# Expert results gathered with an add, transfers spread over steps, slots worked out inside units, throw-away matmuls in the last units

## The chip, the cores and the metric

The kernel runs on one core of a Trainium2 chip. The metric is the device time of the whole launch in microseconds. The core has TensorE (PE in the profile), VectorE (DVE), ScalarE (ACT), GpSimd (POOL) and the queues of DMA transfers that SyncE (SP), ACT and POOL issue.

## The reference

x has 4 sequences of 1024 rows of 128. The result is x + attention(xn) + experts(xn), with xn the layer norm of x.

```python
xn = _layernorm(x)
# attention: 16 heads of 8, rotary embedding, causal softmax, output projection Wo
# experts, 8 of them, 512 wide:
probs = softmax(xn @ router_w.T); top_w, top_idx = top_k(probs, 2)
top_w = top_w / (sum(top_w) + 1e-09)
y_e = relu(xn @ w1[e].T + b1[e]) @ w2[e].T + b2[e]
out = sum over the two chosen experts of top_w * y_e
```

All of it is in float32.

## The kernel before

**Start.** x is loaded and normalised into `xn_all`, transposed, projected to q, k, v and to the router's logits, for the four sequences in turn. DVE then chooses two experts per row (L937 to L947) and computes their shares and the gates (L949 to L954). PE counts the tokens of each expert (`count_tokens`), and DVE turns the counts into the slot of every row in a list sorted by expert, each expert's part rounded up to whole tiles of 128 rows (L1098 to L1124). The list has 72 tiles, in DRAM (`slots_in_d`).

**Units.** Attention is cut into 16 units, one per sequence and group of four heads. `unit(u, r)` on each engine walks through 12 steps, a step being one block of 128 keys against one half (512) of the queries: 4 steps for the first half, 8 for the second. In step j PE makes the scores of step j + 2 (L1271), ACT their exponentials into one of three tiles `probs` (L764), POOL masks the diagonal block in steps 0 to 3 and 8 to 11 (L660), and PE makes the products with the values (L1306). In between, `plan_items` spreads 20 items of the maximum search of the next two units: PE makes raw scores (L1237), DVE takes their maxima (L874, L882). After step 6 DVE joins the maxima, PE transposes them in step 7 (`turn_max`, `TURN` is 7), DVE copies them out (L991) and SP stores them as two more rows of the next unit's stack (`store_max_rows`, L418). DVE copies the head results out at steps 3 and 11 (L997).

**Transfers in units.** POOL scatters the 64 blocks of 128 rows of xn (32 blocks, two experts each) into their slots with indirect DMAs (L634), in units 0 to 11. The table `SCATTERS` says how many stand behind which of the eight masks: three behind the mask of step 3 in units 0 to 3, two in units 4 to 11, and some single ones.

**Experts.** Behind unit 11 (`LAST` is 12) the 72 tiles run: SP loads a tile, PE transposes it (L1364), multiplies with the expert's first weights (L1355), ACT and DVE add the bias and clip, PE multiplies with the second weights (L1373), DVE copies the result (L1062), and SP stores it (L536). PE and ACT have made the first two steps of unit 12 before that. At tiles 0, 3, 68 and 70 SP loads x anew into `acc`, which is the memory of `xn_all` (`load_acc`, `ACC_AT`). POOL waits for all stores of results in `before_last`, ahead of unit 12.

**Units 12 to 15.** POOL gathers the results back, 64 indirect DMAs of 128 rows into eight tiles `got` (L643, table `TRANSFERS`, up to 12 of them behind the mask of step 3), and waits before each for the combine of eight earlier. DVE multiplies each with its share and adds it to `acc` (`combine`, L1029, table `COMBINES`). Sums and heads of the sequences are spread and multiplied (`invert_sums`, `finish_heads`), PE projects them in unit 15 (`project`, L1396, L1410), DVE adds the projection to `acc` (L1045), and SP stores.

**Warm matmuls.** `keep_warm(n, to)` issues n matmuls whose result nobody reads (L1159); `WARM` has their numbers at six places of the start.

## Time and profile before

| | us |
|---|---|
| median of 3 runs | 768.5 |
| lowest, highest | 759.3, 769.29 |
| profiled execution, as timed | 764.56 |
| its span in the profile | 762.8 |
| PE busy | 696.3 |
| DVE busy | 582.2 |
| ACT busy | 444.4 |
| POOL busy | 254.8 |

Busy is the time with an instruction of the engine under way. PE's pipelined matmuls make its figure an upper one. "Idle before" names what ended an engine's idle time; "issue" and "remote" mean that the profile shows no wait that explains it.

### The profile page before, as it was taken

To read this page: it belongs to the slowest core of one execution; us is meant where nothing else is said; L and a number is where in the kernel's file an instruction comes from. 1 tells how busy PE (TensorE), PEld (TensorE's weight loads), DVE (VectorE), ACT (ScalarE), POOL (GpSimd) and SP (SyncE) were. 2 spreads that over 40 slices of the span, in tenths; PEclk is the share of its full clock that TensorE was granted. 3 is DMA by queue.
4 is the path that set the end of the run, shared out by engine and by line. 5 is a ranking of instruction groups with operands and counts; after the bars stand their busy time and mean duration, and the time that the engine had idled before them with its cause. 6 is when DMAs were issued, how large, how long until landed. Compare 5 with 4: busy or idle time off the path is not lost. (4 is left out here: it accounts for less than half of the span.)

```text
span 762.8 us, 18457 instructions
## 1 busy us (share of the span) xinstructions
PE 696.3 (91%) x6064; PEld 398.4 (52%) x6064; DVE 582.2 (76%) x1337; ACT 444.4 (58%) x962; POOL 254.8 (33%) x308
## 2 busy tenths in 40 slices
PE   8799898999999999999999997999999779788887
PEld 3456343434434444444444447999999624343434
DVE  6956978879879889889889884666666559797344
ACT  3455024666666677677677675666666346556541
POOL 2556212424334333433523520000000146565821
PEclk9999998999999999999999998999999869898989
DMA  8499950236355255134225413222222521111654
GB/s 222 129 231 231 236 100 20 45 78 102 73 116 100 60 96 80 38 54 79 50 45 77 63 32 95 78 69 69 69 69 69 135 52 38 46 34 40 162 126 130
DMA packets 64621, 69.36 MB, mean 91 GB/s; under 512 B 9934, under 2 KB 52430, under 8 KB 64490
## 3 DMA queue, kind: packets, MB, share of 16 engines
q1 hardware_dynamic: 60458, 60.08, 36.2%
q0 software_dynamic: 4096, 8.40, 4.2%
q8 instruction: 40, 0.66, 0.4%
q14 instruction: 27, 0.22, 0.1%
HBM read 41.11 MB, written 26.67 MB: 89 GB/s over the span
## 5 line engine op out<-in xcount | busy, mean ns | idle before, releaser
L764 ACT ACTIVATE probs<-bank 128x512 f32<-128x512 f32 (+2 forms) x640 | 314.8, 555 | 214.0 <-PE bank L1271 185.1
L882 DVE TENSOR_REDUCE mx<-bank 128x2 f32<-128x1024 f32 (+2 forms) x200 | 220.6, 1130 | 51.1 <-PE bank L1245 33.8
L1271 PE MATMUL bank<-stack 64*128 64x512 f32 (+3 forms) x768 | 196.4, 439 | 25.8 <-issue 16.0
L660 POOL TENSOR_SCALAR_AFFINE_SELECT probs<-probs 128x512 f32<-128x512 f32 x128 | 81.1, 635 | 406.7 <-ACT probs L764 253.6
L1306 PE MATMUL bank<-probs,vst 128*32 128x256 f32 (+2 forms) x2560 | 199.6, 387 | 5.0 <-POOL probs L660 5.0
L1271 PEld LDWEIGHTS bank<-stack 64*128 64x128 f32 x768 | 89.9, 189 | 157.5 <-issue 77.7
L1237 PE MATMUL bank<-stack 64*128 64x512 f32 (+3 forms) x768 | 149.2, 382 | 6.1 <-DVE mx L882 4.0
L874 DVE CUSTOM_DVE_ANT_0 q_high<-bank,later_s 128x384 bf16<-128x384 f32 (+1 forms) x240 | 135.1, 619 | 9.5 <-PE bank L1237 8.0
L1306 PEld LDWEIGHTS bank<-probs,vst 128*32 128x32 f32 x2560 | 52.2, 110 | 88.9 <-issue 72.7
L1237 PEld LDWEIGHTS bank<-stack 64*128 64x128 f32 x768 | 78.0, 193 | 39.1 <-issue 19.6
L1355 PE MATMUL bank<-tiles_s,staged 128*128 128x128 f32 x576 | 78.3, 280 | 0.7 <-ACT tiles_s L768 0.7
L1373 PE MATMUL bank<-staged,q_high 128*128 128x128 f32 x576 | 76.2, 275 | 0.5 <-DVE k_high L1062 0.5
L643 POOL DMA_INDIRECT k_high<-slots_out_d,slot x64 | 61.3, 958 | 40.6 <-DVE xn_all L1029 27.3
L1355 PEld LDWEIGHTS bank<-tiles_s,staged 128*128 128x128 f32 x576 | 71.4, 195 | 1.4 <-ACT tiles_s L768 1.4
L1373 PEld LDWEIGHTS bank<-staged,q_high 128*128 128x128 f32 x576 | 70.0, 192 | 0.7 <-issue 0.6
L778 ACT COPY staged<-early 128x516 f32 x72 | 44.8, 622 | 42.8 <-DVE q_high L1071 41.4
L634 POOL DMA_INDIRECT slots_in_d<-xn_all,slot x64 | 62.6, 977 | 12.8 <-issue 12.8
L1071 DVE TENSOR_SCALAR q_high<-bank,staged 128x128 f32<-128x128 f32 x144 | 43.9, 346 | 23.7 <-PE bank L1355 20.4
L789 ACT ACTIVATE q_high<-bank,staged 128x128 f32<-128x128 f32 x144 | 44.6, 360 | 1.6 <-PE bank L1373 1.1
L1062 DVE COPY k_high<-bank 128x128 f32<-128x128 f32 x72 | 21.0, 292 | 27.7 <-PE bank L1373 27.7
L997 DVE COPY xnT<-bank 128x512 f32<-128x512 f32 x32 | 22.0, 687 | 17.4 <-remote 10.3
L1159 PE MATMUL bank<-ones_b 128*128 128x512 bf16 x122 | 32.1, 415 | 1.1 <-POOL ones_b L586 1.1
(137 smaller groups left out, 477.4 us busy)
## 6 DMA issues: line engine op xcount, KB each, us to landing
stack<-parts_d SPq DMA_DIRECT2D x96, 128.0 KB
slots_in_d<-const_s SPq DMA_DIRECT2D x4, 1152.0 KB, 10.5
tiles_s<-slots_in_d SPq DMA_DIRECT2D x72, 64.0 KB, 1.8
slots_out_d<-k_high SPq DMA_DIRECT2D x72, 64.0 KB, 1.6
early<-in_w_experts SPq DMA_DIRECT2D x8, 514.0 KB
stack<-parts_d SPq DMA_DIRECT2D x64, 64.0 KB
parts_d<-probs SPq DMA_DIRECT2D x8, 512.0 KB, 6.1
heads_d<-xnT SPq DMA_DIRECT2D x124, 18.0 KB
```

The lines of the kernel that those rows point to most:

```text
L634: pool.indirect_dma_start(out=slots_in_d, out_offset=bass.IndirectOffsetOnAxis(ap=slot[:, k2, t:t + 1], axis=0), in_=xn_all[:, t, :], in_o ...
L643: pool.indirect_dma_start(out=got[n % GOT], out_offset=None, in_=slots_out_d, in_offset=bass.IndirectOffsetOnAxis(ap=slot[:, k2, t:t + 1], ...
L660: pool.affine_select(out=t, in_=t, compare_op=ALU.is_ge, fill=0.0, base=0, pattern=[[0, HG], [1, P]], channel_multiplier=-1).then_inc(s["d ...
L764: nc.scalar.activation(to, src, ACT.Exp, scale=SCALE).then_inc(s["probs_made"], 1)
L778: nc.scalar.copy(w_s[r % 2][:, 0:F + FC], early[:, bass.ds(e * WIDE, F + FC)]).then_inc(s["w1_staged"], 1)
L874: last = v.tensor_tensor_reduce(hidden_scores[n % 2 * 2 + g][:, 0:w], ms[(r * MI + n) % 2][:, g * HALF:g * HALF + w], later_s[:, HALF - w: ...
L882: v.tensor_reduce(to, src.rearrange("p g (a k) -> p g a k", k=w), AX_X, ALU.max, negate=True).then_inc(s["scores_read"], 1)
L1237: last = mm(at[:, col:col + w], qstk[r][g][:, hp, qb * P:(qb + 1) * P], kstk[r][g][:, hp, c * HALF:c * HALF + w], start=not both or i == 0 ...
L1271: made = mm(st_of(u, n, i)[:, col:col + HALF - q0], kstk[r][g][:, hp, kb * P:(kb + 1) * P], qstk[r][g][:, hp, c * HALF + q0:(c + 1) * HALF ...
L1306: last = mm(pv[32 * h:32 * h + 32, begin:end], vst[r % 2][:, kb, h, :], probs[n % 3][:, h, begin:end], start=kb == 0 and begin == 0, stop= ...
L1355: last = mm(at[:, col:col + P], w_s[r % 2][:, f * P:(f + 1) * P], xtT[r % 2], start=True, stop=True)
L1373: last = mm(pv[:, 0:C], hid[r % 2][:, f * P:(f + 1) * P], w_s[r % 2][:, F + FC + f * C:F + FC + (f + 1) * C], start=f == 0, stop=f == FC - 1)
```

## The change

- *Adding gathers.* The share of each row travels with the row: `xn_all` becomes the first 128 columns of `rows_s`, whose column 129 holds the share. `put_share(0)` fills it for the first expert's scatters and `put_share(1)`, in unit 6, for the second's. DVE's copy of an expert's result multiplies with that column. The gathers add into `acc` themselves (`compute_op=ALU.add`); `combine`, `got` and the semaphore `combined` go. The gather of a row's second expert waits until that of the first has landed, and `add_projection` waits for the gathers of its sequence (`results_added`).
- *Paced transfers.* POOL waits at every step, not at masked ones alone, for the step's probabilities, and `SCATTERS` and `TRANSFERS` have an entry for each of 12 steps: one scatter per step in units 2 to 11, two gathers per step in steps 3 to 8 of units 12 to 15. The wait for all stored results stands before the first gather.
- *Slots in units.* The chain from the counts to the slots, the shares and the gates runs in pieces (`rank`) behind the reads of steps 7 to 10 of units 0 to 3 and 6. The transposes of the gates (`turn_gates`) move to the front of the experts.
- *Tile loads.* The first four stand in unit 11, before the store of the second half's heads. A later tile is loaded behind the store of the tile before, three ahead.
- *Maximum rows of unit 0.* Half of them are stored on ACT's queue.
- *Throw-away matmuls.* `WARM` is smaller at two places; there is one behind each early score of unit 0, three at the experts' front, three before the last `turn_max`, and two at most steps from (14, 8) on (`FILLS`).

```diff
@@ -313,7 +314,7 @@
-        WARM = [30, 45, 1, 10, 22, 6]
+        WARM = [30, 35, 1, 10, 12, 6]
@@ -320,16 +321,18 @@
+        FILLS = {**{(LAST + 2, j): (7, 0) for j in range(TURN + 1, NS)}, **{(LAST + 3, j): (7, 0) for j in range(5)},
+                 **{(LAST + 3, j): (4, 1) for j in range(6, 8)}, **{(LAST + 3, j): (7, 2) for j in range(9, NS)}}
-        INVERTS = {4: 0, 5: 1, 7: 2}
+        INVERTS = {8: 0, 9: 1, 10: 2}
-        SCATTERS = [[1, 0, 0, 3, 1, 0, 0, 1]] * 4 + [[1, 0, 0, 2, 1, 0, 0, 1]] * 8
+        SCATTERS = ([[0] * 12] * 2 + ([[0, 0, 0, 1, 1, 1, 1, 1, 1, 0, 0, 1]] * 4 + [[0, 0, 1, 1, 1, 1, 0, 0, 0, 0, 0, 0]]) * 2)
-        TRANSFERS = [[1, 0, 0, 11, 2, 1, 0, 2]] * 2 + [[1, 0, 0, 12, 2, 1, 0, 2]] + [[1, 0, 0, 9, 2, 0, 0, 0]]
-        COMBINES = [[0, 0, 1, 0, 1, 2, 3, 3, 2, 1, 1, 1], [0, 1, 1, 0, 2, 2, 3, 3, 2, 1, 1, 1],
-                    [0, 1, 1, 0, 2, 3, 3, 3, 2, 1, 1, 1], [1, 1, 1, 0, 1, 2, 2, 2, 2, 1, 1, 0]]
+        TRANSFERS = [[0, 0, 0, 2, 2, 2, 2, 2, 2, 1, 1, 2], [1, 0, 0, 2, 2, 2, 2, 2, 2, 1, 1, 2],
+                     [1, 0, 0, 2, 2, 2, 2, 2, 2, 1, 1, 2], [1, 1, 1, 2, 2, 2, 2, 2, 1, 0, 0, 0]]
...
@@ -348,7 +351,7 @@
-            return n // 4 * 2 + n % 2, n // 2 % 2
+            return n // 8 * 4 + n % 4, n // 4 % 2
...
+                if isinstance(u, int) and u == LAST - 1:
+                    sp.wait_ge(s["scattered"], 16 * 2 * NT)
+                    for j in range(4):
+                        load_tile(j, j)
                 store_heads(u, 1)
...
             def tile(j, r):
                 if past(j):
                     store_tile(j - 1, (r - 1) % 4)
-                if not isinstance(j, int) or j + 4 < TILES:
-                    sp.wait_ge(s["xT_made"], j + 1)
-                    load_tile(j + 4, r)
+                    if not isinstance(j, int) or j + 3 < TILES:
+                        load_tile(j + 3, (r + 3) % 4)
...
             def gather(n):
                 t, k2 = gather_order(n)
-                if n >= GOT:
-                    pool.wait_ge(s["combined"], n - GOT + 1)
-                pool.indirect_dma_start(out=got[n % GOT], out_offset=None, in_=slots_out_d,
+                if n == 0:
+                    for r in range(4):
+                        pool.wait_ge(y_stored[r], 16 * TILES // 4)
+                if k2 == 0:
+                    pool.wait_ge(acc_loaded[t // T], 16)
+                else:
+                    pool.wait_ge(gathered[(n - 4) % GOT], 16 * ((n - 4) // GOT + 1))
+                pool.indirect_dma_start(out=acc[:, t, :], out_offset=None, in_=slots_out_d,
                                         in_offset=bass.IndirectOffsetOnAxis(ap=slot[:, k2, t:t + 1], axis=0),
+                                        compute_op=ALU.add).then_inc(gathered[n % GOT], 16)
...
+                    else:
+                        pool.wait_ge(s["probs_made"], banks_before(u, n + 1))
+                    if u < LAST:
+                        for i in share_of(SCATTERS, u, n):
+                            scatter(i)
+                    else:
+                        for i in share_of(TRANSFERS, r, n):
+                            gather(i)
...
@@ -1059,7 +1057,7 @@
-                v.tensor_copy(yst[r % 4], pv[:, 0:C]).then_inc(s["y_copied"], 1)
+                v.tensor_scalar(yst[r % 4], pv[:, 0:C], tile_rows[:, r % 4, C:C + 1], None, ALU.mult).then_inc(s["y_copied"], 1)
...
+            def rank(u, j):
+                if (u, j) == (0, TURN):
+                    first_slots()
+                if (u, j) == (0, TURN + 1):
+                    next_slots()
+                if (u, j) == (0, TURN + 2):
+                    places()
+                if (u, j) == (1, TURN):
+                    slots_of(0)
+                if (u, j) == (1, TURN + 2):
+                    slots_of(1)
+                if (u, j) == (1, TURN + 3):
+                    share_out()
+                    put_share(0)
+                if (u, j) == (6, TURN + 2):
+                    put_share(1)
+                if (u, j) == (2, TURN + 2):
+                    gates_out()
+                if (u, j) == (3, TURN):
+                    expert_tiles()
+                if (u, j) == (3, TURN + 2):
+                    expert_ends()
...
                     if j == TURN and more(u, 1):
+                        if not more(u, 2):
+                            pe.wait_ge(s["scores_read"], UNITS * MI - 2)
+                            keep_warm(3, 7)
                         turn_max(u + 1, (r + 1) % 4)
                     second_products(r, j)
+                    if (u, j) in FILLS:
+                        to, read = FILLS[u, j]
+                        pe.wait_ge(s["scores_read"], UNITS * MI + read)
+                        keep_warm(2, to)
...
@@ -1386,8 +1456,11 @@
                 turn_tile(0, 0)
+                turn_gates()
+                keep_warm(3, 7)
                 all_tiles(pe, tile)
...
@@ -1433,11 +1506,13 @@
-            pe.wait_ge(s["gT_kept"], 1)
+            pe.wait_ge(s["scores_read"], MI + AT_START)
             for n in range(LEAD):
                 for h in range(HG):
                     score(0, 0, n, h)
-            pe.wait_ge(s["routed"], 1)
+                    if n or h:
+                        keep_warm(1, 7)
+            pe.wait_ge(s["counts_kept"], 2)
```

## Rows read from the trace of the kernel before

**Rows 1.** The page: the span, and the granted clock in 40 slices

```profile
span 762.8 us, 18457 instructions
...
PEclk9999998999999999999999998999999869898989
```

**Rows 2.** Busy time by unit: length, PE, PEld, DVE, ACT, POOL, clock, DMA

```profile
147.70:177.90 30.20, 28.19 (x275) 12.41 (x274) 24.73 (x53) 19.64 (x41) 11.21 (x15) 0.94 0.39 74
177.90:206.70 28.80, 26.79 (x278) 12.19 (x277) 24.54 (x53) 19.71 (x41) 11.27 (x16) 1.00 0.56 98
206.70:236.90 30.20, 28.27 (x277) 12.57 (x276) 24.77 (x53) 19.67 (x41) 11.23 (x16) 0.94 0.45 91
...
320.20:347.80 27.60, 26.74 (x274) 12.15 (x273) 24.51 (x53) 19.54 (x41) 10.24 (x15) 1.00 0.38 59
...
607.20:646.50 39.30, 33.71 (x273) 14.14 (x273) 27.68 (x59) 18.71 (x39) 22.58 (x27) 0.80 0.27 49
646.50:682.30 35.80, 29.41 (x274) 13.14 (x274) 31.48 (x73) 20.13 (x41) 21.70 (x27) 0.90 0.17 43
682.30:716.70 34.40, 28.11 (x234) 11.80 (x233) 24.10 (x59) 19.79 (x40) 22.09 (x27) 0.90 0.24 61
716.70:752.30 35.60, 31.05 (x257) 16.00 (x256) 12.45 (x22) 15.88 (x32) 15.68 (x19) 0.90 0.64 160
...
461.80:603.30 141.50, 139.65 (x1225) 138.64 (x1225) 92.37 (x287) 93.60 (x286) 0.00 (x0) 0.99 0.27 78
```

**Rows 3.** Order of time, third scatter of unit 1: start, length, [idle before]

```profile
154.28 0.96 POOL L634 DMA_INDIRECT slots_in_d<-xn_all,slot  x1 [0.30 <-issue]
...
156.07 0.69 DVE L997 COPY xnT<-bank 128x512 f32<-128x512 f32 x1 [1.04 <-remote]
```

**Rows 4.** Order of time, second and last scatter of unit 4

```profile
242.24 0.96 POOL L634 DMA_INDIRECT slots_in_d<-xn_all,slot  x1 [0.30 <-issue]
```

**Rows 5.** Order of time, gathers of unit 14 beside DVE, ACT and PE

```profile
690.21 0.95 POOL L643 DMA_INDIRECT k_high<-slots_out_d,slot  x1 [0.30 <-issue]
...
692.19 0.69 DVE L997 COPY xnT<-bank 128x512 f32<-128x512 f32 x1 [1.54 <-remote]
...
692.88 1.33 ACT L764 ACTIVATE probs<-bank 128x512 f32<-128x512 f32 x2 [2.68 <-remote]
...
693.53 0.49 PE L1271 MATMUL bank<-stack 64*128 64x512 f32 x1 [2.79 <-issue]
```

**Rows 6.** Page, gathers: busy, mean ns, idle before; and the combines alone

```profile
L643 POOL DMA_INDIRECT k_high<-slots_out_d,slot x64 | 61.3, 958 | 40.6 <-DVE xn_all L1029 27.3
...
L1029 DVE SCALAR_TENSOR_TENSOR xn_all<-k_high,share,xn_all x64: 253/344/731, 618.1 to 752.0; 128x128 f32<-128x128 f32 x64
```

**Rows 7.** Order of time, end of the start

```profile
86.25 0.18 DVE L949 SCALAR_TENSOR_TENSOR r_s<-share 128x32 f32<-128x32 f32 x1
...
89.06 0.42 DVE L957 COPY tiles_s<-bank 128x256 f32<-128x256 f32 x1 [0.60 <-PE bank L1219]
...
98.11 2.55 PE L1159 MATMUL bank<-ones_b 128*128 128x512 bf16 x11
...
101.30 0.41 DVE L1098 COPY staged<-bank 128x256 f32<-128x256 f32 x1
...
101.46 2.50 SPq L418 DMA_DIRECT2D stack<-mrow  x4
...
106.83 0.73 PE L1271 MATMUL bank<-stack 64*128 64x512 f32 x3
...
109.02 0.20 DVE L1124 TENSOR_SCALAR expert<-xnT 128x72 int32<-128x72 f32 x1
```

**Rows 8.** Order of time, experts' first transpose; chain, a later load

```profile
461.03 0.45 PE L1364 MATMUL bank<-const_s,tiles_s 128*128 128x128 f32 x1 [3.49 <-DMA tiles_s<-slots_in_d]
...
474.98 3.05 DMA tiles_s<-slots_in_d
```

**Rows 9.** Order of time, unit 12's first products

```profile
607.18 1.08 PE L1306 MATMUL bank<-probs,vst 128*32 128x256 f32 x8 [3.21 <-POOL probs L660]
```

**Rows 10.** Chain of waits, the last gathers of unit 15

```profile
743.87 6.74 DMA k_high<-slots_out_d,slot
```

More of the change, by code:

```diff
@@ L795, in experts @@
                 act.wait_ge(s["experts_loaded"], 16 * E)
+                act.wait_ge(s["expert_known"], 1)
                 stage_w1(0, 0)
@@ L1124, in _, with put_share @@
[L1124 to L1128 removed]
+                if n:
+                    dve.sem_inc(s["routed"], 1)
+            def put_share(n):
+                if n:
+                    dve.wait_ge(s["scattered"], 16 * NT)
+                v.tensor_copy(rows_s[:, :, C], share[:, n, :]).then_inc(s["shared"], 1)
```

189 lines of the change are left out of this document (93 added, 96 removed).

## The prediction

> **What bounds the kernel now.** I read the page first, then the busy time unit by unit, then the order of instructions where a unit is long, and last the two stretches in which one stage hands over to the next. The page says that the profiled execution took 762.8 us of span, and its clock line has dips behind the expert stage [rows 1]. The unit-by-unit view shows what matters most. Unit 7 takes 27.6 us with TensorE (PE) busy 26.74, VectorE (DVE) 24.51, GpSimd (POOL) 10.24 and the clock at 1.00: PE bounds a steady unit. Units 12, 13 and 14 take 39.3, 35.8 and 34.4 us for the same products, at clocks of 0.80 and 0.90 (of the full 2.4 GHz), and unit 15 takes 35.6. Units 1, 2 and 3 take 30.2, 28.8 and 30.2. The 72 expert tiles take 141.5 us between unit 11 and unit 12, with PE busy 139.65 [rows 2].
>
> What makes units 1 to 3 and 12 to 14 long is seen where POOL issues transfers in a row. In unit 1 a third scatter starts at 154.28 and DVE's copy of the heads, which waits for PE's fourth step, comes only at 156.07, after 1.04 us in which what it waited for should long have been done [rows 3]. In unit 4 only two scatters stand there, and nothing is late [rows 4]. In unit 14 gathers follow each other every 1.25 us; ACT sits for 2.68 us and PE for 2.79 us right behind them [rows 5]. After such a hold the clock falls to 1.2 GHz for a stretch, which is how unit 14 comes to a mean of 0.90. Units 12 to 14 also carry 64 combines of 344 ns on DVE [rows 6]; unit 13 has DVE busy 31.48 us [rows 2], more than a steady unit lasts. Both are causes, and the trace doesn't separate them.
>
> **The change part by part.** The sum is made against the profiled execution, 764.56 us as it was timed (762.8 of span and 1.8 around it). The median of the runs shown is 768.5, four above it.
>
> *Before the first unit.* The share and gate work, from L949 at 86.25 to L957's end at 89.48, leaves DVE's path: 3.2 us, of which PE still needs some for the counts and its first item. I take 2.1. The four stores of the maximum rows are 2.50 us of SP's queue [rows 7]; two of them move to ACT's queue, so the last is issued 1.2 earlier. Together -3.3 (0 to -4.4). The slot work behind (L1098 to L1124, 101.30 to 109.22) runs beside PE's warm matmuls and the wait for those rows until 106.83 [rows 7], so its going gives nothing more. The warm matmul that now follows each early score is 0.23 us (2.55 by 11) [rows 7]; seven of them lie behind ACT's exponentials. Unit 0 has 18 score reads in its first seven steps and is DVE's; I leave it.
>
> *The same work inside units 0 to 3 and 6.* 3.2 plus 7.9 us, some 11 us of DVE, go into units in which DVE has 27.6 less 24.5, or 3.1 us free [rows 2]. The pieces stand at steps 7 to 11, where PE next waits for DVE's reads. None of it may show, or all 11 may; units 0 and 1 get most of it, over 3 us each. I take +4.
>
> *Scatters one per step.* A scatter occupies POOL for some 0.96 us [rows 4] and one alone or two in a row delay nothing. Units 1 to 3 lose their excess over 27.6: 2.6, 1.2 and 2.6 [rows 2], -6.4 (0 to -6.4). The 64 scatters now stand one to a step in units 2 to 11, seven in a full unit, where POOL has 17 us free. The wider rows (129 columns for 128) I cost at nothing: they hide behind PE, and a tile load now is issued two tiles, 3.8 us, before its turn; without that cover each of 72 tiles would show it.
>
> *Entering the experts.* PE's first tile starts at 461.03 after 3.49 us of waiting for the first tile's load [rows 8]. The loads move into unit 11, ahead of SP's store of heads. Two transposes and three warm matmuls come in, about 1.1. So -2.4. One later load took 3.05 behind the 512 KB load of x [rows 8]; the acc loads remain, and I take -1 (0 to -2). Scaling the result by its weight in DVE's copy is hidden: PE is busy 139.65 of 141.5 [rows 2].
>
> *Leaving the experts.* PE waits 3.21 us before the first products, since POOL held the mask of step 0 until all results were stored [rows 9]. That wait moves to the first gather, at step 3, behind the masks: -3.2. Late next are the gathers, and nobody wants those before unit 15.
>
> *Units 12 to 15.* Over three steady units, units 12 to 14 have 39.3 + 35.8 + 34.4 - 82.8 = 26.7 us too much [rows 2]. The combines go (64 times 0.344, 22 us of DVE), and so does POOL's waiting for them, 27.3 us [rows 6]. What stays: POOL. A gather is 0.96 plus 0.3, 1.25 us [rows 5]; 17 a unit make 21.3, and with masks and the v copy (10.24 less five scatters, 5.4) 26.7 of 27.6 us. It fits, barely, and now waits at each step for its probabilities, which can push a mask late. I take +2 for each of three units, +6. In units 14 and 15, 31 warm matmuls of 0.23 are 7.2 us of PE, about half of it where PE waits anyway: +3. The second gather of a row waits for the first to land. Under load one took 6.74 us [rows 10], and two steps are some 4.6: +2. Unit 15 is 35.6 with three projections in it; I give it -2. So -26.7 - 2 + 6 + 3 + 2 = -17.7.
>
> Sum: -3.3 + 4 - 6.4 - 2.4 - 1 - 3.2 - 17.7 = -30.0, and 764.6 less 30 is 735 (-4.4% on the median).
>
> The largest term rests on how POOL's transfers and PE disturb each other. The row shows PE sitting for 2.79 us beside a run of gathers [rows 5]. The Trainium skill (SBUF — State Buffer, Who interferes with whom) says the opposite: PE and ACT never wait on anyone, and DMA has ports of its own. By the rows pacing is worth most of 26.7 and 6.4; by the rule it is worth nothing in itself, and only the combines' departure counts. The rule is a rival below.
>
> **The accumulating gather** is not in the trace. Its nearest row is the plain gather, 958 ns [rows 6]. From below it costs that. From above I take twice, 1.9 us (plus the 0.3 between two), since it names the same rows and each row is read twice, once from each side. I take the plain price: POOL writes one list of 128 rows either way.
>
> **The rivals.**
>
> *A, the run remains a run.* Two gathers at each of six steps of 2.2 to 2.5 us are again one every 1.25 us, so PE can be held as in unit 14. For: the cadence is that of [rows 5]. Against: nothing but POOL's short waits between pairs. A hold of 2.8 and its slow-clock stretch (a clock of 0.90 over 34.4 us is 6.9 us at 1.2 GHz, at most 3.4 us lost) are 5 to 6 us a unit, less the 2 already in the sum: +11, 746. If also the lone scatter that now falls on PE's fourth step holds it by 1.2 in nine units, 757.
>
> *B, everything is hidden.* No late masks, no cost of the slot work: -6 - 4, so 725; with fills and landings hidden, 720.
>
> *C, gathers don't disturb PE.* Pacing then gives nothing: units 1 to 3 keep their 6.4, and units 12 to 14 gain what DVE loses, 17 combines of 0.344, 5.9 us each, 17.6, without the other terms of POOL. -3.3 + 4 - 2.4 - 1 - 3.2 - 17.6 + 3 = -20.5: 744. For: DVE's 31.48 in unit 13 [rows 2]. Against: DVE too sat idle there, 1.54 us [rows 5].
>
> *D, slower: the accumulating gather is dear.* POOL is full at 1.3 us per gather. Each further 0.1 costs 64 of them 6.4 us. It eats the 30 us from 1.3 + 30/64, some 1.8 us on, and is slower by 2% from 2.1. At 1.9 + 0.3 the sum is 735 + 0.9 x 64, or 793. Masks are the victims: steps 8 to 11 and 0 to 3 would wait for POOL.
>
> **How the numbers follow.** Forecast 735 (728 to 741): 0.38. A (742 to 757): 0.25. B (below 728): 0.19. C (744): 0.08. D: 0.10. The range takes the forecast, A, B and C whole: 715 to 757. Two per cent is about what a measurement of this kernel tells from no change; faster by that is below 753. So faster 0.84, same 0.08, slower 0.08.
>
> **What would show it.** Right: units 1 to 3 near 27.6; units 12 and 13 under 31 at a clock near 1.00; first products right behind the last result; gathers of 0.96 us in pairs. Wrong: a gather row well above 1 us (D); ACT and PE idle together at the fourth step beside gathers (A); units 0 and 1 longer by 3 us at steps 7 to 11 (the slot work). My largest doubt is the 2 us per unit for late masks.

## The result, and the profile after

| | before | after |
|---|---|---|
| median of the runs made together | 768.9 us (4 runs) | 785.9 us (4 runs) |
| span of the profiled execution | 762.8 us | 791.6 us (timed as 793.4) |

The changed kernel is slower: the ratio of the mean times is 1.026, 95% interval 1.017 to 1.036, so whether it is slower by as much as 2% stays open. Medians and ratios below are of the fast runs, since a slow execution of the same kernel takes some per cent longer. The page's first lines say where to look: a clock that is lower behind the experts than before (compare [rows 1]), nearly three times the packets in GpSimd's queue for the same kind of gather, gathers of 1575 ns for 958 [rows 6], and, in the chain of waits, the load of an expert tile at 4%, which has 1% in the page of the kernel before.

Page of the kernel after: span, granted clock, GpSimd's queue, chain by line, gathers:

```profile
span 791.6 us, 18396 instructions
...
PEclk9999967998999999999999999999999986959799
...
q0 software_dynamic: 11264, 8.43, 6.7%
...
PE bank L1369 6%; PE bank L1443 5%; PE bank L1334 5%; DMA k_high<-slots_in_d 4%; POOL rows_s L655 2%; PE bank L1300 2%; ACT q_high L795 2%; PE bank L1425 2%; ACT probs L770 2%; PE bank L1434 2%; ACTq L778 1%; SPq L541 1%; PE bank L1218 1%; DVE k_high L1060 1%; PE bank L1469 1%
...
L655 POOL DMA_INDIRECT rows_s<-slots_out_d,slot x64 | 100.8, 1575 | 20.1 <-issue 11.0
```

Kernel after, busy time by stretch, columns as in [rows 2]: units 1, 2, 3 and 7, then from unit 11's last product to unit 12's first (the experts with the way in and out), then units 12 to 15:

```profile
152.70:182.40 29.70, 27.06 (x273) 12.30 (x273) 27.44 (x63) 20.11 (x42) 6.18 (x11) 1.00 0.40 62
182.40:213.10 30.70, 29.73 (x273) 13.19 (x274) 25.96 (x56) 18.69 (x39) 11.64 (x16) 0.89 0.50 94
213.10:241.30 28.20, 27.03 (x273) 12.29 (x274) 25.82 (x56) 19.57 (x41) 12.79 (x17) 1.00 0.55 100
324.70:352.40 27.70, 26.83 (x276) 12.17 (x276) 24.63 (x53) 19.63 (x41) 12.21 (x17) 1.00 0.39 64
461.20:628.60 167.40, 153.22 (x1249) 142.10 (x1242) 95.86 (x296) 102.38 (x293) 1.27 (x2) 1.00 0.26 68
628.60:666.80 38.20, 29.21 (x278) 13.06 (x277) 25.45 (x56) 20.66 (x42) 29.63 (x25) 0.85 0.45 62
666.80:706.60 39.80, 36.06 (x273) 15.69 (x273) 26.43 (x51) 18.84 (x39) 32.58 (x27) 0.71 0.29 39
706.60:745.10 38.50, 33.00 (x248) 12.79 (x248) 19.88 (x38) 20.33 (x42) 31.46 (x27) 0.78 0.53 103
745.10:780.90 35.80, 33.53 (x275) 16.84 (x276) 7.35 (x7) 14.58 (x30) 27.83 (x21) 1.00 0.56 116
```

The same stretch between unit 11 and unit 12 of the kernel before:

```profile
456.60:607.20 150.60, 141.72 (x1245) 139.72 (x1238) 95.62 (x299) 97.09 (x294) 0.62 (x1) 0.97 0.28 80
```

So the 28.8 us of span divide like this: the first product of unit 0 is 3.2 later (115.4 for 112.2); units 0 to 11 add 1.4; the expert stretch adds 16.8 (167.4 for 150.6); units 12 to 14 add 7.0 (116.5 for 109.5); unit 15 and what follows 0.4. Two things had no term in my sum, the expert stretch growing and the gathers' price.

**Where the expert stretch grows.** The kernel after in order of time, one turn of the tile loop, first on SyncE's queue, then on PE:

```profile
541.71 0.35 SPq L541 DMA_DIRECT2D slots_out_d<-k_high  x1
542.26 0.34 SPq L537 DMA_DIRECT2D k_high<-slots_in_d  x1
...
542.29 0.32 PE L1434 MATMUL bank<-const_s,k_high 128*128 128x128 f32 x1 [0.36 <-ACT q_high L795]
542.57 1.13 PE L1443 MATMUL bank<-staged,q_high 128*128 128x128 f32 x8
543.53 1.06 PE L1425 MATMUL bank<-tiles_s,staged 128*128 128x128 f32 x8
544.43 0.27 PE L1434 MATMUL bank<-const_s,k_high 128*128 128x128 f32 x1
```

L541 stores the result of tile j - 1, L537 behind it loads tile j + 3. The transpose of that tile (L1434) is the one at 544.43: 2.2 us later, and that only since the pitch (the time from one tile to the next) has already grown. A tile load lands 1.8 us after its issue (the page, in both kernels). What the lead would be at the old pitch of 1.9 us can be read from the trace of the kernel before: from the place behind the store of tile j - 1, 0.55 us after that store's issue, to the transpose of tile j + 3 there are 1.54 us (median of tiles 10 to 59; 1.48 to 1.57). That is less than the landing takes, so the loop can't keep its pitch: 58 tiles pass between 470 and 600 us where 68 did before. The lead that the kernel before really gives its loads, four tiles ahead, is 3.44 us in the median; in the kernel after it is 2.06.

**Where units 12 to 14 grow.** Step 7 of these units takes 9.3, 6.3 and 6.3 us where a steady unit has 3.2. Kernel after, unit 13, GpSimd and then PE:

```profile
688.46 1.55 POOL L655 DMA_INDIRECT rows_s<-slots_out_d,slot  x1 [0.30 <-ACT probs L770]
690.32 1.57 POOL L655 DMA_INDIRECT rows_s<-slots_out_d,slot  x1 [0.30 <-ACT probs L770]
691.29 1.25 POOL L672 TENSOR_SCALAR_AFFINE_SELECT probs<-probs 128x512 f32<-128x512 f32 x1
...
692.68 0.79 PE L1369 MATMUL bank<-probs,vst 128*32 128x256 f32 x8 [3.40 <-POOL probs L672]
```

PE stands for 3.40 us for the mask of step 8, and the mask stood behind ten gathers. They come every 1.84 to 1.86 us; the plain ones came every 1.25 [rows 5]. (The mask's record begins inside the last gather's and ends 0.65 us after it, so its 1.25 us are 0.63 of work and the rest of waiting; before it has 0.63. POOL's busy time in the windows above counts such an overlap once, so it is not too large by it.)

### The profile page after: what moved, and what is told of

It is laid out like the page before. It is cut to its first block and busy times, and to the rows that moved or that the text cites. A ratio compares the mean times of both kernels' runs of the same rounds, so it can differ in the third digit from the quotient of the medians.

```text
span 791.6 us, 18396 instructions
## 1 busy us (share of the span) xinstructions
PE 722.3 (91%) x6085; PEld 404.9 (51%) x6085; DVE 565.2 (71%) x1276; ACT 449.8 (57%) x962; POOL 296.1 (37%) x308
## 3 DMA queue, kind: packets, MB, share of 16 engines
q1 hardware_dynamic: 60394, 60.14, 35.4%
q0 software_dynamic: 11264, 8.43, 6.7%
## 5 line engine op out<-in xcount | busy, mean ns | idle before, releaser
L672 POOL TENSOR_SCALAR_AFFINE_SELECT probs<-probs 128x512 f32<-128x512 f32 x128 | 95.8, 763 | 370.3 <-ACT probs L770 369.2
L1369 PE MATMUL bank<-probs,vst 128*32 128x256 f32 (+2 forms) x2560 | 201.8, 391 | 21.0 <-POOL probs L672 19.4
L1334 PEld LDWEIGHTS bank<-stack 64*128 64x128 f32 x768 | 90.7, 194 | 141.6 <-ACT probs L770 68.1
L887 DVE CUSTOM_DVE_ANT_0 q_high<-bank,k_high 128x384 bf16<-128x384 f32 (+1 forms) x240 | 135.2, 620 | 12.5 <-PE bank L1300 10.2
L655 POOL DMA_INDIRECT rows_s<-slots_out_d,slot x64 | 100.8, 1575 | 20.1 <-issue 11.0
L1300 PEld LDWEIGHTS bank<-stack 64*128 64x128 f32 x768 | 79.1, 199 | 40.4 <-issue 18.3
L641 POOL DMA_INDIRECT slots_in_d<-rows_s,slot x64 | 62.2, 973 | 57.2 <-ACT probs L770 52.7
L1443 PE MATMUL bank<-staged,q_high 128*128 128x128 f32 x576 | 79.6, 281 | 0.5 <-DVE k_high L1060 0.5
L1425 PE MATMUL bank<-tiles_s,staged 128*128 128x128 f32 x576 | 76.2, 275 | 0.4 <-ACT tiles_s L774 0.4
L1060 DVE TENSOR_SCALAR k_high<-bank,k_high 128x128 f32<-128x128 f32 x72 | 25.3, 351 | 51.2 <-PE bank L1443 51.2
L1218 PE MATMUL bank<-ones_b 128*128 128x512 bf16 x143 | 43.8, 435 | 1.1 <-POOL ones_b L587 1.1
```

What stands on the lines that cost most here:

```text
L641: pool.indirect_dma_start(out=slots_in_d, out_offset=bass.IndirectOffsetOnAxis(ap=slot[:, k2, t:t + 1], axis=0), in_=rows_s[:, t, :], in_o ...
L655: pool.indirect_dma_start(out=acc[:, t, :], out_offset=None, in_=slots_out_d, in_offset=bass.IndirectOffsetOnAxis(ap=slot[:, k2, t:t + 1], ...
L672: pool.affine_select(out=t, in_=t, compare_op=ALU.is_ge, fill=0.0, base=0, pattern=[[0, HG], [1, P]], channel_multiplier=-1).then_inc(s["d ...
L887: last = v.tensor_tensor_reduce(hidden_scores[n % 2 * 2 + g][:, 0:w], ms[(r * MI + n) % 2][:, g * HALF:g * HALF + w], later_s[:, HALF - w: ...
L1300: last = mm(at[:, col:col + w], qstk[r][g][:, hp, qb * P:(qb + 1) * P], kstk[r][g][:, hp, c * HALF:c * HALF + w], start=not both or i == 0 ...
L1334: made = mm(st_of(u, n, i)[:, col:col + HALF - q0], kstk[r][g][:, hp, kb * P:(kb + 1) * P], qstk[r][g][:, hp, c * HALF + q0:(c + 1) * HALF ...
```

## The experiments

All ratios are to the kernel before as it ran beside them. "Stretch" is from unit 11's last product to unit 12's first. Besides before and after, twelve kernels ran.

| kernel | ratio, 95% interval | stretch | units 12 / 13 / 14 | unit 15, to its last step |
|---|---|---|---|---|
| before | 1 | 150.6 | 39.3 / 35.8 / 34.4 | 35.1 |
| after | 1.026 (1.017 to 1.036) | 167.4 | 38.2 / 39.8 / 38.5 | 35.4 |
| plain_gather | 1.014 (1.005 to 1.022) | 170.2 | 40.4 / 33.6 / 34.7 | 38.1 |
| early_tile_loads | 0.984 (0.977 to 0.990) | 146.0 | 38.4 / 39.0 / 38.4 | 35.1 |
| old_start | 1.024 (1.017 to 1.031) | 170.1 | 37.6 / 37.3 / 38.5 | 34.5 |
| before_paced | 0.972 (0.965 to 0.978) | 146.0 | 33.9 / 36.9 / 35.4 | 33.1 |
| spread_adds | 1.022 (1.013 to 1.032) | 165.6 | 36.7 / 37.7 / 38.1 | 35.0 |
| after_repaired | 0.990 (0.986 to 0.995) | 143.9 | 36.5 / 36.7 / 37.7 | 35.1 |
| no_fills | 1.021 (1.012 to 1.031) | 167.7 | 38.4 / 39.0 / 38.1 | 34.6 |
| gathers_apart | 0.990 (0.983 to 0.997) | 145.2 | 34.0 / 35.4 / 29.4 | 47.1 |
| repaired_plain | 0.981 (0.973 to 0.990) | 144.1 | 33.8 / 34.8 / 36.6 | 33.4 |
| paced_apart | 0.979 (0.970 to 0.987) | 146.0 | 34.0 / 33.9 / 32.1 | 32.9 |
| paced_inverts | 0.982 (0.973 to 0.990) | 145.7 | 35.7 / 37.5 / 35.4 | 31.4 |
| before_late_loads | 1.023 (1.009 to 1.038) | 172.9 | 38.2 / 35.7 / 35.9 | 38.8 |

### The late tile load: early_tile_loads, before_late_loads

early_tile_loads puts the load back to its old place. The weight then no longer lies in the row when the result is copied, so the copy multiplies by a constant column:

```diff
-                    if not isinstance(j, int) or j + 3 < TILES:
-                        load_tile(j + 3, (r + 3) % 4)
+                if not isinstance(j, int) or j + 4 < TILES:
+                    sp.wait_ge(s["xT_made"], j + 1)
+                    load_tile(j + 4, r)
...
-                v.tensor_scalar(yst[r % 4], pv[:, 0:C], tile_rows[:, r % 4, C:C + 1], None, ALU.mult).then_inc(s["y_copied"], 1)
+                v.tensor_scalar(yst[r % 4], pv[:, 0:C], eps_s[:], None, ALU.mult).then_inc(s["y_copied"], 1)
```

> The changed kernel with the tile loads issued as before: four tiles ahead, behind the transpose that frees the buffer. The weight column would be overwritten too early, so the copy multiplies by a constant column instead (the experts' weights are left out of the result); its cost stays. Theory L (in the changed kernel the load is issued so late that PE's transpose of the tile waits for its landing, 1.8 us): the expert stage goes from 167.6 us between the last products of unit 11 and the first of unit 12 to 145 to 150, total lower by 17 to 22 us. Rival M (the copy with a multiply or the rows of 129 columns slow the stage): it stays over 160, total within 1% of the changed kernel.

The stretch falls by 21.4 us and the ratio from 1.026 to 0.984: the kernel now takes less time than the one before, by 1.6%. (The median is 27 us below the changed kernel's, more than the 17 to 22 expected.) Rows of 129 words and the scaled copy (351 ns for 292) are still in it, so these cost nothing that shows.

before_late_loads is the other direction, this one move alone in the kernel before:

```diff
-                if not isinstance(j, int) or j + 4 < TILES:
-                    sp.wait_ge(s["xT_made"], j + 1)
-                    load_tile(j + 4, r)
+                    if not isinstance(j, int) or j + 3 < TILES:
+                        load_tile(j + 3, (r + 3) % 4)
```

> The kernel before with one thing of the change alone: in the experts the load of tile j + 3 behind the store of tile j - 1, instead of the load of tile j + 4 behind the transpose of tile j. Rows of 512 bytes, gathers, slots and start as before. Theory L (the load is issued only some 1.6 us before its transpose at the old pitch, and takes 1.8 us and more to land, so the pitch of a tile goes from 1.9 to about 2.2 us): from unit 11's last product to unit 12's first it takes 170 to 173 us instead of 150.6, and the kernel takes 785 to 790 us, 2.7 to 3.1% above the kernel before. Rival X (it needs the change's other parts too, the row of 129 words whose landing is longer, or the scaled copy of 351 instead of 292 ns in front of the store): 151 to 158 us there, 766 to 774 us in all.

The stretch grows by 22.3 us and the ratio is 1.023. Nothing else of the change is needed; rival X is out. PE's transpose in before_late_loads, grouped from 470 to 600 us (count, busy us and mean ns, idle before and releaser):

```profile
L1363 PE MATMUL bank<-const_s,tiles_s 128*128 128x128 f32 x59 | 18.4, 312 | 4.8 <-DMA tiles_s<-slots_in_d 3.5 <-ACT q_high L788 0.6
```

The same group in the kernel before, which differs from it by this move alone:

```profile
L1364 PE MATMUL bank<-const_s,tiles_s 128*128 128x128 f32 x68 | 18.6, 273 | 0.6 <-DMA tiles_s<-slots_in_d 0.6
```

59 transposes against 68 in the same 130 us. The idle time put down to the load is small, 3.5 us, and yet the load costs 22: a late transpose delays ACT's copy and that the next tile's first products, and a wait on that chain is booked under other names. The stage's length shows the cost, the wait's row does not.

### The adding gather: plain_gather, spread_adds, after_repaired, repaired_plain

plain_gather takes the sum away from the changed kernel (each gather overwrites; the sums are left out):

```diff
-                                        in_offset=bass.IndirectOffsetOnAxis(ap=slot[:, k2, t:t + 1], axis=0),
-                                        compute_op=ALU.add).then_inc(gathered[n % GOT], 16)
+                                        in_offset=bass.IndirectOffsetOnAxis(ap=slot[:, k2, t:t + 1], axis=0)).then_inc(gathered[n % GOT], 16)
```

> The changed kernel with one thing undone: the gathers don't add, they overwrite (the sums of expert results are left out). All waits and places stay. Theory G (the adding gather is what makes units 12 to 14 long: 1549 ns on POOL for 958 before, so the mask of step 8 comes late): gathers fall to about 0.96 us, step 7 of units 12 to 14 from 9.3, 6.3 and 6.3 us to about 3.1, units 12 to 14 from 38.2, 39.8 and 38.5 us to 28 to 30, total lower by 22 to 28 us. Rival H (a run of gathers one every 1.25 us holds PE at the fourth step whatever the gathers do): gathers are short, but step 3 takes 5 to 6 us again, units 33 to 34, total lower by 10 to 15. Rival F (the warm matmuls and waits for landings make them long): no change beyond 1%.

Gathers are 944 ns again (median) and the holds at step 7 shrink from 9.3, 6.3 and 6.3 us to 4.4, 3.1 and 2.9, but units 12 to 14 only fall from 116.5 to 108.7 us, because other holds come: 6.6 us at step 6 of unit 12, 6.7 at step 5 of unit 14. The whole gains 1.2% with intervals that overlap. So theory G's 22 to 28 us didn't come, and not even rival H's 10 to 15, though long steps beside runs of gathers are what H is about.

spread_adds keeps the sum and takes the ten gathers in five steps apart:

```diff
-        TRANSFERS = [[0, 0, 0, 2, 2, 2, 2, 2, 2, 1, 1, 2], [1, 0, 0, 2, 2, 2, 2, 2, 2, 1, 1, 2],
-                     [1, 0, 0, 2, 2, 2, 2, 2, 2, 1, 1, 2], [1, 1, 1, 2, 2, 2, 2, 2, 1, 0, 0, 0]]
+        TRANSFERS = [[1, 1, 1, 1, 2, 2, 1, 1, 1, 2, 2, 1], [1, 1, 1, 1, 2, 2, 2, 1, 1, 2, 2, 1],
+                     [1, 1, 1, 1, 2, 2, 2, 1, 1, 2, 2, 1], [1, 1, 1, 1, 2, 2, 2, 1, 1, 2, 0, 0]]
```

> The changed kernel with another table of gathers: one in the steps 0 to 3 and 8, two in the steps 4 to 6, where POOL has no masks, 16 to 17 in a unit instead of 16 to 18, and no ten in the five steps 3 to 7. Experts and all else as in the changed kernel. Theory S (the adding gather's 1.55 us is dear only because ten of them stand in a row in front of the mask of step 8): POOL has 17 x 1.6 + 8 masks x 0.6 = 32 us of work in a unit and PE's own is 34, so the hold at step 7 (6.3 to 9.3 us of a step) goes, units 12 to 14 take 34 to 35.5 us each instead of 38.2, 39.8 and 38.5, and the time falls by 10 to 13 us to 773 to 776. Theory F (POOL is full, the place doesn't matter): the hold turns into smaller ones at other masks, units 12 to 14 stay at 37 to 39 us each, and the time is 782 to 788.

The hold at step 7 shrinks to 3.8 to 4.5 us and steps 9 and 10 become 4.1 and 4.2: 112.5 us in place of 116.5, and no gain in the ratio that can be told. Theory F holds: POOL is all but full. The table has 16, 17 and 17 gathers in units 12, 13 and 14 (the 18 in the expectation is one too many). 17 at 1.84, eight masks at 0.63 and the v copy of 0.39 are 36.7 us, and units 13 and 14 take 37.7 and 38.1; besides the 0.3 us between two gathers POOL's idle time in them is 2.0 and 1.9 us. By this only fewer gathers in a unit could shorten it, which was not tried with adding ones.

after_repaired is spread_adds with the early load made right: VectorE copies the weight to a tile of its own, behind which the row may be overwritten:

```diff
+            def keep_weight(j, r):
+                dve.wait_ge(s["xT_made"], j + 1)
+                if not isinstance(j, int) or j >= 4:
+                    dve.wait_ge(s["y_copied"], j - 3)
+                v.tensor_copy(weights[:, r % 4:r % 4 + 1], tile_rows[:, r % 4, C:C + 1]).then_inc(s["weight_kept"], 1)
...
                 if following:
                     stage_w2(j + 1, r + 1, e)
+                    keep_weight(j + 1, r + 1)
```

> The same table of gathers, and the tile loads four ahead again behind the transpose as before, with the weight's column copied by VectorE to a small tile of its own, so that the scaled copy still multiplies the right weight. Theory S with theory L (the late tile load costs the experts 20 to 27 us): the experts take 142 to 147 us and units 12 to 14 take 34 to 35.5 each; 745 to 750 us, 2.5 to 3% below the kernel before. Theory F with L: 755 to 760. If the wider row itself (516 instead of 512 bytes) or the small copies cost something, experts come out above 147 us, as early_tile_loads (145.9) had both the wide rows and no small copies.

759.0 us, ratio 0.990, against 1.022 for spread_adds beside it: a stretch of 143.9 us for 165.6. Against the kernel before that is no difference of 2%. The 72 small copies (148 ns each) hide. With theory F I had expected 755 to 760; this is all of the change, repaired.

repaired_plain is that kernel with plain gathers (sums left out again):

> after_repaired with the gathers plain again (the sums are left out: every gather overwrites the row of x, so this is a price and no kernel to use). The traces so far show an adding gather every 1.84 us when POOL has nothing else to do (1.54 of the gather, 0.3 to the next) and a plain one every 1.25. Theory F (POOL is full in units 12 to 14: 18 x 1.84 + 8 masks x 0.63 + 0.4 = 39 us in the changed kernel): with plain gathers POOL needs 17 x 1.25 + 5.4 = 27 us, its idle time comes back, the steps of 4.1 to 4.5 us at 7, 9 and 10 fall to 2.1 to 3.2, units 12 to 14 take 32 to 34.5 us each instead of 36.5, 36.7 and 37.7; 745 to 752 us. Theory R (runs of plain gathers hold PE, as in plain_gather, whose units 12 to 14 took 40.4, 33.6 and 34.7): the table has at most six gathers in three steps, so one step of 4 us or more stays in every unit, at 5 to 6, and the time is 752 to 758.

750.8 us; units 12 to 14 take 105.2 us for 110.9 and unit 15 33.4 for 35.1. So the adding costs 7.4 us in these units; the ratios, 0.981 and 0.990, give the same 7 with intervals that overlap. POOL has room now, but steps of 5.3, 5.5 and 6.0 us stand at 7, 5 and 5: theory R has its part (the time lies in F's range, the long steps and unit 14 in R's). Busy time of units 12 and 14 in after_repaired; POOL's number, the last but three, is what to look at:

```profile
605.40:641.90 36.50, 31.70 (x277) 13.93 (x277) 25.69 (x52) 20.08 (x41) 30.95 (x26) 0.82 0.47 66
...
678.60:716.20 37.60, 31.05 (x245) 12.26 (x244) 19.52 (x37) 19.54 (x41) 32.60 (x26) 0.82 0.52 99
```

The same units in repaired_plain:

```profile
597.90:631.70 33.80, 30.17 (x276) 13.38 (x275) 24.28 (x51) 19.76 (x41) 21.62 (x27) 0.90 0.37 70
...
666.50:703.10 36.60, 32.51 (x245) 12.93 (x244) 18.84 (x38) 19.30 (x40) 20.85 (x26) 0.83 0.25 61
```

### Pacing by itself: before_paced, gathers_apart, paced_apart, paced_inverts

before_paced is the kernel before (plain gathers, combines on VectorE, its own start) with at most two transfers in a row, the wait for the results moved from all masks to the first gather, and the first four tile loads in unit 11:

```diff
-        SCATTERS = [[1, 0, 0, 3, 1, 0, 0, 1]] * 4 + [[1, 0, 0, 2, 1, 0, 0, 1]] * 8
+        SCATTERS = [[1, 0, 0, 2, 1, 1, 0, 1]] * 4 + [[1, 0, 0, 2, 1, 0, 0, 1]] * 8
-        TRANSFERS = [[1, 0, 0, 11, 2, 1, 0, 2]] * 2 + [[1, 0, 0, 12, 2, 1, 0, 2]] + [[1, 0, 0, 9, 2, 0, 0, 0]]
+        TRANSFERS = [[0, 0, 0, 2, 2, 2, 2, 2, 2, 1, 1, 2], [1, 0, 0, 2, 2, 2, 2, 2, 2, 1, 1, 2],
+                     [1, 0, 0, 2, 2, 2, 2, 2, 2, 1, 1, 2], [1, 1, 1, 2, 2, 2, 2, 2, 1, 0, 0, 0]]
```

> The kernel before, with plain gathers and combines kept, and these parts of the change: at most two scatters in a row, gathers two per step at the places of the changed kernel, POOL's wait for all results at the first gather, the first four tile loads in unit 11. The combines follow two steps behind their gathers. Theory P (pacing removes PE's hold, and the two hand-overs save their waits of 3.5 and 3.2 us): units 12 to 14 take 29 to 31 us, units 1 to 3 27.6 to 28.8, total 738 to 746. Rival H (the cadence of one gather every 1.25 us holds PE anyway): step 3 of units 12 to 14 stays at 5 us and more, total 755 to 762. Rival C (DVE with its combines is the bound): units 12 and 13 at 32 or more without a long step 3, total 748 to 755.

750.3 us, ratio 0.972: faster than both kernels. Units 1 to 3 take 27.9, 27.6 and 27.6 us, the stretch 146.0, units 12 to 14 106.1 for 109.5. None of the three theories fits whole: P's 29 to 31 us a unit are missed, H's long step 3 is not there, and C's numbers are met (units over 32 without a long step 3, 748 to 755). But what makes the units long is a hold at step 5 of units 13 and 14 (6.7 and 6.8 us), and C's reason, the combines, doesn't explain it: repaired_plain has no combines and has it too (5.5 and 6.0). before_paced in unit 13: PE's last full pair of scores before the hold, the last of six gathers in a row, then ACT, PE and DVE:

```profile
646.91 0.50 PE L1274 MATMUL bank<-stack 64*128 64x512 f32 x2
...
649.40 0.94 POOL L648 DMA_INDIRECT k_high<-slots_out_d,slot  x1 [0.30 <-issue]
650.40 1.09 ACT L767 ACTIVATE probs<-bank 128x512 f32<-128x512 f32 x2 [3.12 <-remote]
...
651.05 0.75 PE L1274 MATMUL bank<-stack 64*128 64x512 f32 x1 [2.41 <-ACT probs L767]
...
651.73 2.36 DVE L885 TENSOR_REDUCE mx<-bank 128x2 f32<-128x1024 f32 x2 [2.76 <-remote]
```

ACT's input is made by the pair of PE's matmuls of 646.91, which by their rows end at 647.41, 3.0 us before ACT starts. But the profile models a matmul's end, and it records apart from that when a semaphore is raised, the counter by which PE tells ACT that the scores are there. In this trace a score matmul's semaphore rises 0.01 us after the modelled end (median). For this pair it rose at 650.32 and 650.35, and for the products before them (modelled end 646.98) at 650.29; ACT starts at 650.40. So ACT isn't late on an input that is there: it gets PE's word 2.9 us late, and DVE too starts (651.73) right behind a semaphore of PE's (651.70). PE's own wait of 2.41 us, for ACT, comes only after. Whether PE's matmuls themselves stood or only their word did, the trace doesn't tell.

The same can be looked for in all fourteen traces: exponentials that start more than 0.9 us late, with ACT free, their scores made by the modelled end and their buffer free. The eight traces with plain gathers have 52 of them, and in 49 ACT starts within 0.11 us of a semaphore of PE's. The six with adding gathers have none over 0.11 us.

gathers_apart puts one gather in each step of units 12 to 14 and the other 28 in unit 15; the combines follow two steps behind:

```diff
+        TRANSFERS = [[1] * 12] * 3 + [[3, 3, 3, 3, 3, 3, 3, 3, 3, 1, 0, 0]]
+        COMBINES = [[0, 0, 1, 1, 1, 1, 1, 1, 1, 1, 1, 1]] + [[1] * 12] * 2 + [[1, 1, 3, 3, 3, 3, 3, 3, 3, 3, 3, 1]]
```

> before_paced with one gather in every step of units 12 to 14 and the other 28 in unit 15, three in a row; the combines two steps behind. Theory G (a run of plain gathers, one per 1.25 us, holds PE for 2.5 to 3 us when it has gone on for about five of them; a gather that stands alone doesn't): units 12 to 14 have no step of 6.7 us, take 32 to 33.5 us each instead of 33.9, 36.9 and 35.4, and unit 15 has the hold, more than one perhaps. Theory M (the hold is not the gathers but what else lies at those steps: masks, stacks, head stores): a step of over 6 us stays in units 13 and 14 at the same place. The total isn't what this run is for: POOL has 28 x 1.0 us in unit 15 and its last gathers land late; 745 to 756 us.

The three units take 98.7 us for 106.1, 34.0, 35.4 and 29.4 each where theory G had 32 to 33.5, and none of those late semaphores of over 0.9 us is in them; unit 15 has three, of 2.9, 1.3 and 7.9 us. That is what G says. (The units also have fewer gathers and combines than before; repaired_plain's holds without any combine speak against the combines.) The one long step, 5.9 us at step 7 of unit 13, has another cause: PE waits 1.99 us for VectorE's maxima, which stand behind the three reciprocals of the sums (0.94 to 0.96 us each). Unit 15 pays with 47.1 us and one step of 10.9, so the whole gives the gain back.

paced_apart takes a middle way, 15, 15, 16 and 18 gathers, twos with ones between them, and moves the reciprocals to steps 8, 9 and 10; paced_inverts is before_paced with only the reciprocals moved:

```diff
-        INVERTS = {4: 0, 5: 1, 7: 2}
+        INVERTS = {8: 0, 9: 1, 10: 2}
```

> before_paced with 15, 15, 16 and 18 gathers in units 12 to 15, one in most steps and two in three or four of twelve, never in two steps running before unit 14's step 6, and the three reciprocals of the sums in steps 8, 9 and 10 of unit 13 (where the changed kernel has them) instead of 4, 5 and 7. Theory G (five or so plain gathers 1.25 us apart hold PE; single ones don't; and gathers_apart's 5.9 us at step 7 of unit 13 was VectorE's reciprocals in front of the maxima): units 12, 13 and 14 take 32.5, 32 and 31 us instead of 33.9, 36.9 and 35.4, no step over 5 us in them; 738 to 745 us. Theory M: a step over 6 us stays; 748 to 753.

> before_paced with only the three reciprocals moved from steps 4, 5 and 7 of unit 13 to 8, 9 and 10. Theory G: the 6.7 us at step 5 of units 13 and 14 are the runs of gathers, so they stay; VectorE is freer at steps 4 to 7 of unit 13 alone, 0 to 2 us there; 747 to 750 us. Theory V (the reciprocals made the hold of unit 13): unit 13 takes 33 instead of 36.9 us and unit 14 stays at 35; 745 to 748.

paced_apart has no step over 5 us in units 12 to 14, as G said, and they take 100.0 us, between gathers_apart and before_paced. Its profiled span is the shortest of all, 739.9 us, but the median of its four runs is 748.2, above G's 738 to 745, and its interval, 0.970 to 0.987, overlaps with before_paced's: better in the profile, not shown better in time. In paced_inverts steps of 5.1 and 6.5 us at step 5 of units 13 and 14 stay (6.7 and 6.8 in before_paced), so the reciprocals did not make them; units 12 to 14 take 108.6 us and it gains nothing.

### The rest: no_fills, old_start

```diff
-                        if not more(u, 2):
-                            pe.wait_ge(s["scores_read"], UNITS * MI - 2)
-                            keep_warm(3, 7)
                         turn_max(u + 1, (r + 1) % 4)
                     second_products(r, j)
-                    if (u, j) in FILLS:
-                        to, read = FILLS[u, j]
-                        pe.wait_ge(s["scores_read"], UNITS * MI + read)
-                        keep_warm(2, to)
```

> The changed kernel without the throw-away matmuls in units 14 and 15 (two at the end of 16 steps and three in front of unit 15's maxima). Theory W (as in the prediction, they cost PE about 3 us and give no clock back where the clock is full anyway): units 14 and 15 take 38.5 and 35.4 us less 2 to 4 in all, clock in both stretches within 0.05 of the changed kernel's 0.78 and 1.00; 782 to 785 us. Theory K (they keep the clock at its high level in unit 15): without them unit 15 has 5 to 15 us at the low level and takes 2 to 5 us more; 786 to 791. A third outcome is no difference within 0.5%: they lie in time in which PE waits for POOL's masks.

781.0 us. Units 14 and 15 take 1.2 us less in all, at clocks of 0.73 and 0.85 for 0.78 and 1.00. The throw-away matmuls raise the clock somewhat and cost 1 us; in the whole it can't be told from nothing. Theory W's 2 to 4 us are missed, and the clock falls by more than its 0.05, as K has it, but without K's longer time. (They stand at 14 steps, not at 16 as the expectation says.)

```diff
-        WARM = [30, 35, 1, 10, 12, 6]
+        WARM = [30, 45, 1, 10, 22, 6]
...
-                    if n or h:
-                        keep_warm(1, 7)
```

> The changed kernel with the warm matmuls of the start as before (45 and 22, none between the early scores). Theory W (with 12 instead of 22 PE runs dry 3.7 us before the maximum rows land, the clock falls to 1.2 GHz for 17 us, and the matmuls between the scores make each early score take 1.2 us): unit 0's first products come at 110 to 112 us instead of 115.4, unit 0 takes 35 to 36 instead of 37.3, total lower by 5 to 7 us. Rival: the rows' landing at 105.5 us sets it all, total lower by 0 to 2 us.

787.9 us, no gain in the whole. In the profile theory W's first product and unit 0 are there (110.2 us and 36.1 us long; in the profile of after 115.4 and 37.4), but its 5 to 7 us in the time are not. The end of the start in the kernel after:

```profile
98.79 1.45 SPq L421 DMA_DIRECT2D stack<-mrow  x2
...
99.22 2.76 PE L1218 MATMUL bank<-ones_b 128*128 128x512 bf16 x12
105.67 0.57 PE L1334 MATMUL bank<-stack 64*128 64x512 f32 x2 [3.69 <-DMA stack<-mrow]
106.17 0.61 PE L1218 MATMUL bank<-ones_b 128*128 128x512 bf16 x1
106.71 0.79 PE L1334 MATMUL bank<-stack 64*128 64x512 f32 x1
```

The rows are issued 3.7 us before those of [rows 7] are through (100.2 for 104.0), but they land no earlier: the last of the 64 signals of their landing comes at 105.63, in the kernel before at 105.26. There PE's 22 throw-away matmuls ran on until 106.90, so its first scores at 106.83 didn't wait for the rows, and the kernel after starts only 1.2 us earlier. In it the 12 throw-away matmuls run out, PE idles for 3.69 us, the clock is at 1.2 GHz behind it (0.51 over 105.7 to 115.4), and the seven interleaved throw-away matmuls cost 0.61 us each there, not 0.23. In seven profiles with the new start the first product comes at 109.8 to 117.9, mean 113.1; in six with the old one, kernels before, at 111.4 to 114.8, mean 112.9. One profile can't tell a difference of 3 us there.

## Why the prediction was wrong, step by step

I predicted 735 us (715 to 757) and the changed kernel took 785.9.

- **Tile loads: the step that failed.** "A tile load now is issued two tiles, 3.8 us, before its turn", so cost 0. The three of `j + 3` was read as a lead. The load stands behind the store of tile j - 1, which waits for a result that PE makes late in tile j, and its transpose is made in the course of tile j + 2. At the old pitch that leaves 1.5 us for a landing of 1.8. Measured: +21 to +22 us of the stretch, by undoing it in the changed kernel, by undoing it beside spread_adds, and by doing it alone in the kernel before. In whole times the three pairs differ by 4.2, 3.2 and 2.3% of some 768 us, that is by 32, 25 and 18, each give or take some 10. I had the order of SyncE's queue and the landing time in the trace, and the 1.54 us too, and did not put times on them. The sentence behind it, "without that cover each of 72 tiles would show it", was right: 22 over 72 is 0.3 us a tile.
- **Entering and leaving the experts: right.** -2.4, -1 and -3.2, together -6.6. after_repaired has 143.9 us where the kernel before has 150.6: -6.7. The way in (unit 11's last product to the first transpose) goes from 4.46 to 2.10 us, the way out (last transpose to unit 12's first product) from 8.83 to 5.71. The term of -1 is less sure: between them after_repaired gains 1.3, but before_paced, early_tile_loads and paced_apart lose about 1 there and have 146.0 us in all, -4.6.
- **Units 12 to 15: the sign was wrong.** Predicted -17.7; after has +7.3. Two parts. First, the gather's price: "I take the plain price: POOL writes one list of 128 rows either way". It is 1575 ns for 958 in the mean, and rival D's threshold of 1.3 us per gather was passed at 1.84. But D's slope, 6.4 us for each 0.1, would give 35 us, and the adding costs 7.4 (after_repaired against repaired_plain). D reckoned from units of 27.6 us. With plain gathers the real units are 33.8 to 36.6 long (repaired_plain), so POOL, with 26.7 us of work, has 7 to 10 us of slack in each, which the dearer gathers use up first. Second, "26.7 us too much" was taken as won whole by pacing and the combines' going. repaired_plain, which has neither adding nor combines, still takes 105.2 us where the kernel before takes 109.5. That is rival A, with 0.25: two gathers a step remain a run. Rival C, by which gathers don't disturb PE, falls with gathers_apart and with the 52 late semaphores that only kernels with plain gathers have.
- **Slot work and scatters.** Predicted +4 and -6.4. Unit 0 to the end of unit 4 takes 152.3 and 150.1 us in the two profiles of before's schedule, 145.1 to 148.5 in the four paced ones (mean 146.3), and 151.4 to 157.3 in the eight of the changed schedule (mean 153.7). So the pacing (here two scatters in a row at most, not one a step) is worth 5 us, near the 6.4, and the rest of the changed schedule costs 7. I put that down to the slot work, within the bounds of 0 and 11 but above what I took; the wider rows, the scatters' new places and the new start are in it too and were not run apart. Unit 1 and unit 2 show it: 29.7 and 30.7 us, DVE 27.44 and 25.96 for 24.73 and 24.54 [rows 2].
- **The start.** Predicted -3.3, measured 0.2 on the means. The 1.2 us of it for the rows' stores took an earlier issue for an earlier landing, and "the wait for those rows until 106.83" was a misreading: they had landed at 105.26, and PE was in its own throw-away matmuls.
- **Throw-away matmuls.** Predicted +3, measured 1.2 in the profile, not visible in the time.

The sum again with the measured terms, over the kernel before: 0 for the start, +2 for units 0 to 4, -7 for the hand-overs (after_repaired's), +22 for the late load, -6 for units 12 to 15 with plain gathers (138.6 for 144.6) and +7 for the adding: +18. The medians differ by 17. (The profile of after has 151.9 us in units 12 to 15, six more than after_repaired's 146.0. Most of that is the ten gathers in a row: spread_adds, which takes them apart, has 147.5. But it shows no gain in time that can be told.)

What stays open is how a run of plain gathers holds PE. What is shown is only this. Runs of five and more at 1.25 us do it by up to 3.4 us, in before, plain_gather, before_paced, repaired_plain and paced_inverts, and by 7.9 beside ten in a row in unit 15 of gathers_apart; three scatters in a row do it by 1.0 to 1.1 (before, units 1 to 3); one gather a step doesn't (gathers_apart, units 12 to 14), twos with ones between them mostly don't (in units 12 to 14 of paced_apart there are two holds, of 1.8 and 1.9 us), and no adding gather, one every 1.85 us, did it in six traces. What comes late is PE's semaphore, and ACT and DVE wait for that. In before_paced both holds of 3.0 us end within 0.1 us of the end of the last of six gathers. Whether it is the spacing, the number in flight or where the packets go was not tried. By the Trainium skill (SBUF — State Buffer, Who interferes with whom) PE and ACT never wait on anyone. That is a rule about memory ports, and what the runs show is PE's word coming 2.9 us late in before_paced, which needn't be a port's doing. As a forecast that gathers leave PE alone it doesn't hold here.

## What to carry to other kernels

- Give every transfer that you cost at nothing its three times: when its issue can leave the queue (what does the instruction in front of it wait for), when it lands, when it is wanted. A number of buffers is not a lead.
- When an operation that the trace doesn't have goes on an engine that would be full with it, measure it before the rest is scheduled around it. After that, compare the units' length with count times cadence: if they agree, a better order can't help.
- When an engine seems to start late on an input that is there, ask first whether the input's end is modelled. Here the matmul's row said 647.41 and its semaphore 650.35.
- Look at each change of a bundle by itself. Pacing, the hand-overs and nothing else gave 2.8% here; the new gather, the slot work and the start gave nothing, and one moved load took 22 us.

## What the runs showed of the hardware that I had not expected

- An indirect gather that adds into SBUF takes GpSimd 1549 ns in the median (1530 at least), the plain one 944, for the same 128 rows of 512 bytes; its queue moves 11264 packets where plain ones (gathers and scatters together) are 4096. Between two gathers lie 0.30 us in either case.
- A mask issued behind an adding gather is recorded as 1.25 us, 0.6 of which it waits for the gather. The mean in the masks' row of the page is too large by such waits (763 ns for 635); POOL's busy time of 296.1 us is not, as it counts an overlap once (the records add up to 312).
- Beside runs of plain gathers at 1.25 us PE's semaphores come late, by 2.9 us in before_paced, ACT, PE and DVE stand together for 2.4 to 3.1 us, and the clock falls behind it: 0.79 over unit 14 of before_paced, 0.94 in gathers_apart.
- Issuing the rows at the start 3.7 us earlier didn't bring them earlier (105.63 for 105.26): why they landed no sooner was not tried.
